# Four layers on one core: in the first two attentions, who takes the turned outputs out of their bank, and how the sums are inverted

## What is computed

```python
q = (x @ Wq.T).reshape(Bx, Tx, H, dk)          # H = 16, dk = 8, likewise k and v
scores = einsum('bthd,bshd->bhts', q, k) / sqrt(dk)
scores = where(causal_mask, -inf, scores)      # first layer only
out = einsum('bhts,bshd->bthd', softmax(scores), v)
```

## Time and profile before

| | us |
|---|---|
| runs | 3560.81, 3556.45, 3560.78 (median 3560.78) |
| the profiled execution | 3568.88, of it 3567.1 in the span |
| PE busy | 2992.9 (84%) |
| DVE busy | 2607.5 (73%) |
| ACT busy | 2145.6 (60%) |
| POOL busy | 486.4 (14%) |

### The profile page before, as it was taken

How to read it: one execution, slowest core, us unless ns; L and a number is a source line. 1 busy time by engine, 2 the same in 40 slices (tenths; PEclk the granted TensorE clock), 3 DMA queues, 4 the chain that set the end, 5 groups by cost and what they waited for, 6 DMA issues and landing times. The chain is left out here.

```text
span 3567.1 us, 51582 instructions
## 1 busy us (share of the span) xinstructions
PE 2992.9 (84%) x18320; PEld 1209.2 (34%) x18320; DVE 2607.5 (73%) x6022; ACT 2145.6 (60%) x2739; POOL 486.4 (14%) x753
## 2 busy tenths in 40 slices
PE   5999997896999999985999898947569988889836
PEld 2333333443122222214455555535412222222214
DVE  6999973666999999946666666631868888888821
ACT  2566673223377777773555455512479989999812
POOL 2000001333000000004000000013221011102023
PEclk7899998997799999997999999968779999999958
DMA  5442202333211111000000000012362223221112
GB/s 146 62 108 57 33 13 49 66 78 113 28 27 27 23 22 22 12 5 31 1 1 1 7 1 7 1 62 65 104 124 31 31 33 39 31 29 20 53 28 70
DMA packets 172978, 148.30 MB, mean 42 GB/s; under 512 B 79672, under 2 KB 130632, under 8 KB 172720
## 3 DMA queue, kind: packets, MB, share of 16 engines
q1 hardware_dynamic: 168624, 137.21, 19.5%
q0 software_dynamic: 4096, 7.78, 0.7%
HBM read 95.13 MB, written 49.68 MB: 41 GB/s over the span
## 5 line engine op out<-in xcount | busy, mean ns | idle before, releaser
L1324 ACT ACTIVATE a_probs<-a_scores 128x1024 f32<-128x1024 f32 (+3 forms) x896 | 791.4, 932 | 372.2 <-PE a_scores L1206 235.1
L1347 DVE TENSOR_REDUCE a_part_max<-a_slot_ps 128x1 f32<-128x512 f32 x1280 | 798.5, 683 | 32.7 <-PE a_slot_ps L1184 31.2
L2219 DVE TENSOR_TENSOR a_probs<-a_logit_ps,a_gate 128x1024 f32<-128x1024 f32 x512 | 602.3, 1219 | 102.6 <-ACT a_gate L2078 99.3
L1184 PE MATMUL a_slot_ps<-a_k_op,a_q_op 48*128 48x512 bf16 (+3 forms) x1792 | 579.8, 380 | 90.0 <-PEq L123 28.1
L2083 ACT ACTIVATE a_probs<-a_probs 128x2048 f32<-128x2048 f32 x256 | 488.0, 1906 | 8.5 <-DVE a_probs L2219 4.3
L1206 PE MATMUL a_scores<-a_q_op,a_k_op 51*128 51x512 bf16 (+3 forms) x1792 | 453.3, 362 | 7.1 <-ACT a_probs L1324 6.1
L1226 PE MATMUL a_o_ps<-a_probs,a_v_op 128*32 128x512 f32 (+3 forms) x3584 | 438.6, 561 | 1.2 <-ACT a_o_sb L1311 0.6
L1184 PEld LDWEIGHTS a_slot_ps<-a_k_op,a_q_op 48*128 48x128 bf16 x1792 | 150.2, 94 | 692.5 <-DVE a_part_max L1347 469.4
L1984 PE MATMUL a_logit_ps<-space 96*128 96x512 bf16 x1024 | 303.8, 387 | 73.6 <-DVE a_probs L2219 62.8
L2078 ACT ACTIVATE a_gate<-a_diff_ps 128x1024 f32<-128x1024 f32 x256 | 261.3, 1021 | 59.3 <-PE a_diff_ps L1984 51.3
L1997 PE MATMUL a_o_ps<-a_probs,a_v_op 128*32 128x512 f32 x2048 | 275.7, 610 | 7.0 <-DVE a_o_sb L2212 3.1
(11 more groups left out here) (401 smaller groups left out, 3928.0 us busy)
## 6 DMA issues: line engine op xcount, KB each, us to landing
e_coef<-coef_dram SPq DMA_DIRECT2D x16, 1024.0 KB, 10.1
a_q_op<-scratch_q SPq DMA_DIRECT2D x384, 32.0 KB
a_k_op<-scratch_k SPq DMA_DIRECT2D x384, 32.0 KB
scratch_q<-p_parts SPq DMA_DIRECT2D x24, 384.0 KB, 3.3
scratch_k<-p_parts SPq DMA_DIRECT2D x24, 384.0 KB, 3.5
space<-scratch_k SPq DMA_DIRECT2D x192, 32.0 KB
space<-scratch_g SPq DMA_DIRECT2D x192, 32.0 KB
space<-scratch_q SPq DMA_DIRECT2D x192, 32.0 KB
```

The lines of the kernel that those rows point to most:

```text
L1184: nc.tensor.matmul(out[:, 0:width], q_op[g][r0:r0 + MAX_ROW, e, qt * P:(qt + 1) * P], k_op[g][r0:r0 + MAX_ROW, e, kh * CH:kh * CH + width] ...
L1324: nc.scalar.activation(probs[gs % NB][:, 2 * e:2 * e + 2, off:CH], scores[e][:, :, off:CH], ACT.Exp, scale=scale).then_inc(probs_done, 1)
L1347: nc.vector.tensor_reduce(part_max[u % 2][:, kh, col:col + 1], slot[:, 0:w], axis=AX.X, op=ALU.max).then_inc(slot_done, 1)
L2219: nc.vector.tensor_tensor(probs[gs % 4][:, m, :, :], logit_ps[m][:], gate[gs % 2][:], op) \
```

## The change

After the four transposes, ACT copies what is needed of the bank (8 features and the sum of 4 heads of 4 blocks: 144 of the 512 columns) to a new SBUF tile `o_rows`, and the bank is free when that copy is done. Both halves of a unit go to one tile. DVE then takes the inverse of both halves' sums in one operation over 128x32 from SBUF (`inverse_sums`, with the floor before it in a1), and POOL multiplies both halves' rows in one operation over 128x256 from SBUF.

In the queues: ACT's copy of half 1 of the unit before stands after its first exponential (e = 0) of step 3, and that of half 0 after its first exponential of step 7 in a0 and of step 11 in a1, so each in the step after the transposes. DVE's `inverse_sums` stands behind its slots of step 4 of the next unit. POOL's multiplication of unit u - 1 stands after its splitting and its copy of values for unit u. PE's order does not change; only what releases a bank does.

```diff
         def bank_for(n):
             if n >= BANKS:
-                te.wait_ge(slot_done, n - BANKS + 1)
+                wait_used(te, n - BANKS)
...
+        def wait_used(engine, n):
+            by_scalar = shape.by_scalar[n + 1]
+            if by_scalar > shape.by_scalar[n]:
+                engine.wait_ge(rows_copied, by_scalar)
+            else:
+                engine.wait_ge(slot_done, n + 1 - by_scalar)
...
+            def normalise(u):                                   # on gpsimd
+                b, g = u // GROUPS, u % GROUPS
+                pool.wait_ge(rec_done, u + 1)
...
+                nc.gpsimd.tensor_tensor(out, o_rows[u % 2][:, :, :, 0:shape.hd],
+                    rec[u % 2][:].unsqueeze(3).to_broadcast([P, 2 * CPT, H, shape.hd]), ALU.mult).then_inc(rows_done, 1)
...
+                if u > 0:
+                    normalise(u - 1)
+            normalise(UNITS - 1)
...
+            def copy_rows(u, hq):                               # on scalar
+                n = shape.place["o", u, hq]
+                act.wait_ge(slot_ready, n + 1)
+                if u >= 2:
+                    act.wait_ge(rows_done, u - 1)
+                nc.scalar.activation(o_rows[u % 2][:, hq * CPT:(hq + 1) * CPT, :, :],
+                                     slot_ps[n % BANKS][:].rearrange("p (t j v) -> p t j v", t=CPT, j=H)[:, :, :, 0:shape.hd + 1],
+                                     ACT.Copy).then_inc(rows_copied, 1)
...
                         nc.scalar.activation(probs[gs % NB][:, 2 * e:2 * e + 2, off:CH], scores[e][:, :, off:CH],
                                              ACT.Exp, scale=scale).then_inc(probs_done, 1)
+                        if e == 0 and n == 3 and u > 0:
+                            copy_rows(u - 1, 1)
+                        if e == 0 and n == shape.half_end[0] + 4:
+                            copy_rows(u, 0)
             copy_out(UNITS - 1, 1)
+            copy_rows(UNITS - 1, 1)
...
-            def normalise(u, hq):                               # on vector
...
+            def inverse_sums(u):
+                dve.wait_ge(rows_copied, 2 * (u + 1))
+                if u >= 2:
+                    dve.wait_ge(rows_done, u - 1)
+                sums = o_rows[u % 2][:, :, :, shape.hd]
                 if floor:
+                    nc.vector.tensor_scalar(rec[u % 2][:], sums, floor, None, ALU.max).then_inc(floored, 1)
+                    dve.wait_ge(floored, u + 1)
+                    sums = rec[u % 2][:]
+                nc.vector.reciprocal(rec[u % 2][:], sums).then_inc(rec_done, 1)
...
-                    if n == 2 and u > 0:
-                        normalise(u - 1, 1)
-                    if n == shape.half_end[0] + 3:
-                        normalise(u, 0)
+                    if n == 4 and u > 0:
+                        inverse_sums(u - 1)
...
-            normalise(UNITS - 1, 1)
+            inverse_sums(UNITS - 1)
```

More of the change, by code:

```diff
@@ L1005, in __init__ @@
         self.n = len(self.steps)
-        self.place = {}
+        self.place, self.by_scalar = {}, [0]
         for key in self.slot_order():
             self.place[key] = len(self.place)
+            self.by_scalar.append(self.by_scalar[-1] + (key[0] == "o"))
     def off(self, hq, kb):
@@ L1108, in narrow_attention @@
         o_sb = [sb(f"o_sb{i}", [P, CH]) for i in range(2)]
-        rec = [sb(f"rec{i}", [P, CPT, H]) for i in range(2)]
+        rec = [sb(f"rec{i}", [P, 2 * CPT, H]) for i in range(2)]
+        o_rows = [sb(f"o_rows{i}", [P, 2 * CPT, H, shape.hd + 1]) for i in range(2)]
         part_max = [sb(f"part_max{i}", [P, 2, H * KB]) for i in range(2)]
@@ L1124, in narrow_attention @@
         scores_ready, probs_done, pv_done = sem("scores_ready"), sem("probs_done"), sem("pv_done")
-        o_copied, rec_done = sem("o_copied"), sem("rec_done")
+        o_copied, rows_copied, floored, rec_done, rows_done = (
+            sem(n) for n in ("o_copied", "rows_copied", "floored", "rec_done", "rows_done"))
         block = ctx.enter_context(nc.Block())
@@ L1275, in _ @@
         def _(pool):
+            def normalise(u):
+                b, g = u // GROUPS, u % GROUPS
+                pool.wait_ge(rec_done, u + 1)
+                out = (ctx_nat[:, b * KB * feats:(b + 1) * KB * feats].rearrange("p (t f) -> p t f", f=feats)[:, :, g * 32:(g + 1) * 32]
+                       .rearrange("p t (j d) -> p t j d", d=shape.hd))
+                nc.gpsimd.tensor_tensor(out, o_rows[u % 2][:, :, :, 0:shape.hd],
+                                        rec[u % 2][:].unsqueeze(3).to_broadcast([P, 2 * CPT, H, shape.hd]), ALU.mult).then_inc(rows_done, 1)
             nc.gpsimd.memset(zeros[:], 0.0).then_inc(pool_step, 1)
@@ L1288, in _ @@
                 out = max_parts[u % 2]
-                pool.wait_ge(slot_done, shape.place["max", u, 0] + 1)
+                wait_used(pool, shape.place["max", u, 0])
                 if u >= 2:
@@ L1350, in row_maxima @@
             def row_maxima(u):
-                dve.wait_ge(slot_done, shape.place["slot", u, NA - 1] + 1)
+                wait_used(dve, shape.place["slot", u, NA - 1])
                 nc.vector.tensor_tensor(row_max[:], part_max[u % 2][:, 0, :], part_max[u % 2][:, 1, :],
@@ L1363, in negate @@
                                         ALU.mult).then_inc(slot_done, 1)
-            def normalise(u, hq):
[L1367 to L1371, removed]
-                if floor:
[L1373 to L1385, removed]
+            def inverse_sums(u):
[3 more added lines that the diff above has]
+                sums = o_rows[u % 2][:, :, :, shape.hd]
+                if floor:
+                    nc.vector.tensor_scalar(rec[u % 2][:], sums, floor, None, ALU.max).then_inc(floored, 1)
+                    dve.wait_ge(floored, u + 1)
+                    sums = rec[u % 2][:]
+                nc.vector.reciprocal(rec[u % 2][:], sums).then_inc(rec_done, 1)
             for s in range(NA):
```

## The result

The changed kernel takes 3607.01 us (median of 4 runs, 3597.68 to 3611.73), the one before 3560.80 in the same rounds. The ratio is 1.012, interval 1.0106 to 1.0134: slower by 46 us, where 3609 was forecast. The profiled execution is the quickest of the four, 3597.68 us.

What follows compares the result with a forecast made beforehand. The prediction took DVE to set a1's pace, with PE about 0.05 us of slack a step. Late bank 17.6 + 15.0, inverse 8.0 + 4.8 and ends 2.7 made 48.1 us: 3617 profiled, 3609 median, range 3585 to 3630.

Steps and rivals of the forecast that it cites:

- The late bank: PE late by 0.63 us at a1's steps 3 and 11, 0.15 and 0.92 at a0's 3 and 7: 17.6, 15.0 us.
- The inverse: DVE's inverse between the reduces of steps 4 and 5 adds 0.57 us a unit in a1, 0.34 in a0.
- the 0.05 of slack: In a1, PE has about 0.05 us to spare in a step; any longer delay is a hole in DVE.
- POOL: POOL's 128x256 multiplication, starting in step 5, takes 0.73 us and is hidden before its next maxima.
- The sum: 48.1 us on the profiled execution's 3568.88 gives 3617; median of the runs 3609, 1.4% slower.
- both ends: Last unit's copies 0.5 us a layer, uncovered chain at the very end 0.85 a layer: 1.0 and 1.7 us.
- (a): Relieving the full DVE decides, so faster: 3544 us; needs the exponential not to stand ahead of the copy; 5%.
- (b): PE or DVE has unseen slack; inverses and half the lateness stay: 3593 us, or 3580 with inverses hidden; 13%.
- (c): ACT's copy of nine columns out of 32 is slow, 0.60 us, at 56 places: 17.4 us more, 3626; 10%.
- (d): POOL's larger operation slows DVE, at worst blocking it for 0.73 us 28 times: 20 us, 3629; 3%.
- (e): The copy changes nothing, because the bank is wanted later than read: 3561 us; 3%.

Runs made afterwards that it cites:

- the doubled product: Changed kernel with POOL's 128x256 multiplication done twice, the first into a tile nobody reads: 3606.44 us, ratio 1.0132.
- the half-0 run: Changed kernel with ACT's copy of half 0 alone moved ahead of the exponential, half 1 left behind it: 3581.24 us, ratio 1.0025.

## Why the prediction held, point by point

*The late bank.* The copy's price was taken as 0.29 us and is 0.28; nine columns out of 32 cost no more than contiguous ones. It started 0.92 after its exponential, and PE went on 1.90 after the step's first slot (1.94 by the prediction's rows), with 1.29 idle, and reached the next step after 3.44 (3.49 forecast). That leaves 0.57 us late for each place in a1, against 0.63: the unit's 1.47 less the inverse's 0.33, halved. In a0 the two places with copy and inverse cost 1.15 a unit; less the inverse's 0.20 that is 0.95, against 1.07.

*The inverse.* This term was mis-sized, by more than any other: 0.33 us a unit in a1 and 0.20 in a0, against 0.57 and 0.34. I had added durations and gaps. But the floor starts while the last reduce ends, and the next reduce starts before the inverse ends, as here in the changed kernel:

```profile
1230.99 0.17 DVE L1410 TENSOR_SCALAR a_rec<-a_o_rows 128x32 f32<-128x32 f32 x1
...
1231.19 0.35 DVE L1413 RECIPROCAL a_rec<-a_rec 128x32 f32<-128x32 f32 x1
...
1231.46 0.63 DVE L1385 TENSOR_REDUCE a_part_max<-a_slot_ps 128x1 f32<-128x512 f32 x1
```

From 1230.99 to 1231.46 the two hold the place for 0.47, not 0.62. Less the 0.05 of slack that would be 0.42, and the unit shows 0.33; where the other 0.09 went is not shown.

*POOL.* Hidden, as the doubled product shows. It took 0.63 us, not 0.73.

*The sum.* 14 x 1.47 + 14 x 1.15 = 36.7 us, against 45.4 in the prediction (17.6 + 15.0 + 8.0 + 4.8). The two attentions together grew by 43.7 in the profiled pair. Two units of a0 with a lower clock gave 2.0, which the prediction did not have at all: it took the clock as steady. Of the other 5 us, 1.6 lie in the last distance of a0, where the clock fell a third time: 30.46 us at a granted clock of 0.94, against 28.88 at 1.00 with two products. The remaining 3.4 lie in the first and last units and at both ends, for which it had 2.7; I did not part them further. So the total came closer than its terms, and that was partly luck: the bank's terms were 3.3 us too large and the inverse's 5.4, and the clock, which the prediction left out, gave back 3.6.

*The rivals.* (a), the relieved engine, needed the copy to come before the exponential. With the copy there it is faster indeed, 0.9985, and 0.9952 with the inverse in a hole: the rule of the Trainium skill (Perfetto Trace Analysis, Optimizing Scalar/DVE Operations) holds in these runs once the place is right, and in the changed kernel's order the bank outweighed it. (b) does not hold: the half-0 run shows both places of a1 at full price. (c) is ruled out by the copy's 0.28, (d) by the doubled product, (e) by the waits.

## What to carry to other kernels

When an engine is full and another has time to spare, ask where in the other's queue the moved work will stand, and what the instruction ahead of it waits for. Here ACT had a quarter of its time free, but behind the exponential the copy of 0.28 us cost some 0.95 us more in a1 than ahead of it, where it filled a wait. Rotating buffers turn such a delay into everyone's: find the instruction that next needs the buffer, and count back from it. And short work for a full engine goes where that engine waits anyway, not where it is next in order.

## What the runs showed of the hardware

Between the first and the last unit of each attention the lengths and TensorE's granted clock go together without an exception, in all the kernels: a unit as short as the table has it had a clock of 1.00 throughout, and each one longer by 0.2 us or more had a stretch at 1.2 GHz instead of 2.4. Four windows of the changed kernel's a0, 330 to 450 us, hold the two units of 30.63 us (359.69 to 420.95):

```profile
330.00:360.00 30.00, 26.18 (x266) 10.41 (x265) 25.75 (x84) 19.89 (x29) 2.89 (x7) 1.00 0.19 33
360.00:390.00 30.00, 26.77 (x264) 10.72 (x265) 24.96 (x83) 19.52 (x28) 2.26 (x6) 0.94 0.15 33
390.00:420.00 30.00, 26.55 (x262) 10.33 (x260) 25.57 (x83) 19.70 (x28) 2.58 (x6) 0.94 0.22 33
420.00:450.00 30.00, 26.40 (x270) 10.68 (x268) 25.39 (x83) 19.70 (x28) 2.57 (x6) 1.00 0.24 33
```

In both a short part was granted 1.2 GHz, and each was 0.99 us longer than its neighbours. The kernel with the inverse moved alone has the same waits of PE for the copy (1.3 us) and all its units of a0 at 29.44 or 29.45, so at this length of wait it does not always fall. And it fell without such a wait: with the product on VectorE PE waited 0.7 us at most for a slot in a0, and the clock fell in four of its units. So longer waits of PE went with more falls where the copy was made longer (1.3, 1.6 and 2.1 us), but they are not the whole condition, and why the clock falls in one unit and not in the next stays open.
